# The output projection Wo of an attention kernel, from full fp32 matmuls to three float32r terms, with its units and the FFN rounds at other steps

## The reference

```python
q, k, v = x @ Wq, x @ Wk, x @ Wv                # 16 heads of 64
attn = softmax(causal(q @ k.T / 8))
y = x + concat_heads(attn @ v) @ Wo             # Wo: 1024 x 256
y = layernorm(y, eps=1e-3) * gamma + beta
x = layernorm(x + y)                            # eps 1e-5
h = silu(x @ wg.T) * (x @ wu.T)                 # 768 wide, int weights / 127
out = layernorm(x + h @ wd.T)
```

## Time and profile before

| | |
|---|---|
| median of 3 runs | 1461.75 us (1459.99 to 1463.49) |
| the profiled execution: its own time | 1462.12 us |
| the profiled execution: its span | 1459.7 us |
| mean granted TensorE clock | 0.991 |
| PE, PEld busy | 1403.6 us (96%), 1227.6 us (84%) |
| DVE, ACT, POOL busy | 1014.0, 1003.8, 1003.9 us (69% each) |
| DMA queue q1 | 108.94 MB, 25.0% of 16 engines' span |

### The profile page before, as it was taken

The page is one execution under the profiler, slowest core; times in us unless marked ns, Lnnn a source line. Parts: engine busy times, 40 slices in busy tenths (PEclk is TensorE's granted clock), DMA queues, the critical chain, the costliest instruction groups (busy, mean ns, idle before and its releaser), DMA issues.

```text
span 1459.7 us, 23745 instructions
## 1 busy us (share of the span) xinstructions
PE 1403.6 (96%) x7936; PEld 1227.6 (84%) x7936; DVE 1014.0 (69%) x2729; ACT 1003.8 (69%) x1924; POOL 1003.9 (69%) x944
## 2 busy tenths in 40 slices
PE   6999999999999999999999999999999999999876
PEld 5788888888888888888888888888888888888766
DVE  7766666766666676776667676776766667677874
ACT  4776777767676676766668676686867668676534
POOL 4676766666686775868668586785868668587744
PEclk9999999999999999999999999999999999999988
DMA  4333222312342221321232122132223223122000
GB/s 135 97 81 96 64 60 95 116 52 68 108 131 72 61 88 53 90 85 44 88 116 95 52 59 68 59 117 55 78 66 102 88 59 95 52 59 59 23 11 30
DMA packets 61241, 110.45 MB, mean 76 GB/s; under 512 B 16256, under 2 KB 41600, under 8 KB 61120
## 3 DMA queue, kind: packets, MB, share of 16 engines
q1 hardware_dynamic: 61120, 108.94, 25.0%
HBM read 60.95 MB, written 13.89 MB: 51 GB/s over the span
## 4 chain that ended last, share of the span: by engine, by line
PE 81%; DVE 9%; POOL 4%; ACT 3%; issue 2%; DMA 1%; ACTq 0%; SPq 0%; POOLq 0%
PE bank L787 24%; PE bank L760 16%; PE bank L660 12%; PE bank L736 9%; PE bank L723 7%; PE bank L685 5%; PE bank L822 5%; PE bank L834 3%; POOL probs_lo L1403 2%; DVE K L1121 1%; DVE max_part L1156 1%; POOL h_lo L1445 1%; DVE bank L1154 1%; ACT probs_hi L972 1%; ACT probs L969 1%
## 5 line engine op out<-in xcount | busy, mean ns | idle before, releaser
L1403 POOL TENSOR_TENSOR probs_lo<-probs,probs_hi 128x512 fp32r<-128x512 f32 x576 | 744.1, 1299 | 401.0 <-ACT probs_hi L972 397.8
L969 ACT ACTIVATE probs<-bank 128x512 f32<-128x512 f32 x576 | 344.4, 598 | 304.4 <-DVE bank L1170 219.5
L760 PE MATMUL bank<-Q,K 128*128 128x512 f32 (+3 forms) x1536 | 385.3, 352 | 5.2 <-ACT probs_hi L972 4.5
L972 ACT ACTIVATE probs_hi<-bank 128x512 fp32r<-128x512 f32 x576 | 342.6, 595 | 0.0
L760 PEld LDWEIGHTS bank<-Q,K 128*128 128x128 f32 x1536 | 252.8, 190 | 33.6 <-ACT probs_hi L972 5.7
L736 PE MATMUL bank<-K,Q 128*128 128x512 f32 (+3 forms) x768 | 245.6, 362 | 8.4 <-DVE max_part L1154 6.3
L1154 DVE CUSTOM_DVE_ANT_0 bank<-bank,mask_keys_free 128x128 f32<-128x128 f32 (+3 forms) x512 | 243.3, 506 | 3.4 <-PE bank L736 3.0
L787 PE MATMUL bank<-probs_hi,VH 128*128 128x512 f32 (+3 forms) x768 | 232.0, 343 | 6.0 <-POOL probs_lo L1403 5.3
L787 PE MATMUL bank<-probs_lo,VH 128*128 128x512 f32 (+3 forms) x768 | 234.6, 346 | 0.0
L787 PE MATMUL bank<-probs_hi,VL 128*128 128x512 f32 (+3 forms) x768 | 234.4, 346 | 0.0
L1170 DVE TENSOR_TENSOR bank<-bank,mask_queries_free 128x256 f32<-128x256 f32 (+1 forms) x320 | 119.6, 374 | 148.1 <-PE bank L760 147.0
(11 more groups left out here) (170 smaller groups left out, 2224.3 us busy)
## 6 DMA issues: line engine op xcount, KB each, us to landing
Q<-Q SPq DMA_DIRECT2D x64, 256.0 KB, 3.7
K<-K SPq DMA_DIRECT2D x64, 256.0 KB, 3.4
recip_bc<-recip_scratch SPq DMA_DIRECT2D x62, 256.0 KB, 3.4
wh<-w_scratch SPq DMA_DIRECT2D x12, 768.0 KB, 4.9
wl<-w_scratch SPq DMA_DIRECT2D x12, 768.0 KB, 6.6
wo_quad<-wo SPq DMA_DIRECT2D x16, 256.0 KB, 3.2
y<-x SPq DMA_DIRECT2D x16, 256.0 KB, 3.4
x_tail<-x SPq DMA_DIRECT2D x13, 256.0 KB, 3.1
```

Source lines behind the costliest of these rows:

```text
L760: last = mm(bk[:, at:at + cols], KX[:, n, P * i:P * i + P], QX[:, n, q0:q0 + cols], start=(KX is K1 and at == 0), stop=(KX is K2 and at + ...
L969: A(pe_[:, g % 2, :], stb[g % 2][:, :], ACT.Exp).then_inc(exp_done, 1)
L972: A(ph[:, g % RING, :], stb[g % 2][:, :], ACT.Exp).then_inc(hi_done, 1)
L1403: G.tensor_tensor(pl[:, g % RING, :], pe_[:, g % 2, :], ph[:, g % RING, :].bitcast(F32), ALU.subtract).then_inc(lo_done, 1)
```

## The change

Wo's product is made of float32r matmuls in three terms. ACT rounds the quad's Wo and the normed heads, DVE subtracts for the low parts. The heads' parts of one unit (128x512 each) go into the tail's h_hi and h_lo; in iteration 15, where a tail uses them otherwise, into two pairs of buffers carved from xl. A unit is now 12 matmuls of 128x256. The split of a unit stands one step before the unit on both engines. The units of the iterations 1 to 14 move from the steps 12, 14, 15, 21 to 14, 16, 21, 23; the FFN's rounds in STEADY move from up 9, 23, 29 and down 13, 26, 32 to up 9, 24, 30 and down 12, 27, 33. The load of Wo moves from step 23 to 17 of SP's list, its split stands in step 28. The buffer row_sums goes: its uses go to a row of recip_bc and, at the end, to a mask that is no longer needed, with one more wait each. The last quad's units (after iteration 15) stay fp32.

```diff
-WO_AT, WO_AT_LAST = [12, 14, 15, 21], [11, 13, 15, 16]
+WO_AT, WO_AT_LAST = [14, 16, 21, 23], [11, 13, 15, 16]
+WO_LOAD_AT, WO_SPLIT_AT = 17, 28
...
-STEADY = tail_at(-5, -1, 7, [9, 23, 29], [13, 26, 32], 36)
+STEADY = tail_at(-5, -1, 7, [9, 24, 30], [12, 27, 33], 37)
...
-        rsum, RB = sb("row_sums", [P, S]), sb("recip_bc", [P, S])
+        RB = sb("recip_bc", [P, S])
...
+        WoH, WoL = sb("wo_hi", [P, 2, D], F32R), sb("wo_lo", [P, 2, D], F32R)
...
+        def heads_parts(wi, u):
+            return wo_parts[u % 2] if wi == NIT - 2 else (hh[:, :, :], hl[:, :, :])
...
+        def heads_rows(wi, u):
+
+            a, b = sorted([2 * wi % 3, (2 * wi + 1) % 3])
+            return HT[:, a:b + 1:b - a, 2 * P * u:2 * P * u + 2 * P]
...
-            return (misc[1], misc[0], pvb[0], pvb[1])[u] if wi == NIT - 1 else misc[(1, 1, 0, 1)[u]]
+            return (misc[1], misc[0], pvb[0], pvb[1])[u] if wi == NIT - 1 else misc[(u + 1) % 2]
...
-                src = HT[E:E + 1, h // 2 % 3, :] if h % 2 == 0 else rsum[0:1, :]
+                src = HT[E:E + 1, h // 2 % 3, :] if h % 2 == 0 else RB[E:E + 1, :]
...
-                    sp.wait_ge(wo_mm, 4 * it)
+                    sp.wait_ge(wo_lo, it)
...
-                sp.dma_start(rsum[0:E, CH:S], rscr[HA:HA + 1, 0:CH].partition_broadcast(E).rearrange("e o n -> e (o n)")).then_inc(recip_bc, 16)
+                sp.dma_start(RB[0:E, CH:S], rscr[HA:HA + 1, 0:CH].partition_broadcast(E).rearrange("e o n -> e (o n)")).then_inc(recip_bc, 16)
...
+                if s == WO_LOAD_AT and live:
+                    load_wo(it)
...
                 if s == 23 and live:
                     recip_store(QH * it + 1)
-                    load_wo(it)
                 if s == 24 and live:
                     recip_load(QH * it + 1)
...
-                    pe.wait_ge(y_added, 4 * (it - 2) + 2 + u)
+                    pe.wait_ge(y_added, 4 * (it - 2) + 1 + u)
...
-                elif u == 0 and it >= 2:
-                    pe.wait_ge(y_added, 4 * (it - 1))
+                elif it >= 2:
+                    pe.wait_ge(y_added, 4 * (it - 2) + 3 + u)
...
                 elif u == 1:
-                    pe.wait_ge(y_added, 4 * wi + 1)
-                elif u == 2:
                     if running(it):
                         pe.wait_ge(tdve[0], ND * (it - TAIL_LAG) + DV["y20"])
                     else:
                         pe.wait_ge(v_lo, 4 * it + 4)
                 elif it == NIT - 1:
-                    pe.wait_ge(y_added, 4 * wi + 2)
+                    pe.wait_ge(y_added, 4 * wi + u - 1)
                 else:
-                    pe.wait_ge(proj_lo, 2 * proj_unit(it + 1, 0, 2) + 2)
-                if u == 0:
-                    pe.wait_ge(wo_loaded, 16 * (wi + 1))
-                if u % 2 == 0:
-                    pe.wait_ge(ht_norm, 4 * wi + (1 if it == NIT else 3) + u // 2)
+                    pe.wait_ge(proj_lo, 2 * proj_unit(it + 1, 0, u) + 2)
+                if it == NIT:
+                    pe.wait_ge(wo_loaded, 16 * NIT)
+                else:
+                    pe.wait_ge(heads_lo, 4 * wi + u + 1)
+                    if u == 0:
+                        pe.wait_ge(wo_lo, wi + 1)
                 bk = wo_bank(wi, u)
+
+                hi, lo = heads_parts(wi, u)
                 for t in range(2):
                     tok = P * (2 * u + t)
                     for r in range(2):
-                        last = mm(bk[:, D * t:D * t + D], HT[:, (2 * wi + r) % 3, tok:tok + P], WoS[:, r, :],
-                                  start=(r == 0), stop=(r == 1))
+                        if it == NIT:
+                            last = mm(bk[:, D * t:D * t + D], HT[:, (2 * wi + r) % 3, tok:tok + P], WoS[:, r, :],
+                                      start=(r == 0), stop=(r == 1))
+                        else:
+                            a = heads_at(wi, r)
+                            for n, (X, W) in enumerate(((hi, WoH), (lo, WoH), (hi, WoL))):
+                                last = mm(bk[:, D * t:D * t + D], X[:, a, P * t:P * t + P], W[:, r, :],
+                                          start=(r == 0 and n == 0), stop=(r == 1 and n == 2))
                 last.then_inc(wo_mm, 1)
...
+            def wo_split(it):
+
+                act.wait_ge(wo_loaded, 16 * (it + 1))
+                act.wait_ge(wo_mm, 4 * it)
+                A(WoH[:, :, :], WoS[:, :, :], ACT.Copy).then_inc(wo_hi, 1)
+
+            def heads_split(wi, u):
+                if u % 2 == 0:
+                    act.wait_ge(ht_norm, 4 * wi + 3 + u // 2)
+
+                if wi == NIT - 2:
+                    if u == 0:
+                        act.wait_ge(v_mm, 4 * NIT)
+                    act.wait_ge(wo_mm, 4 * wi + max(u - 1, 0))
+                elif u == 0 and running(wi + 1):
+                    act.wait_ge(tpe[0], NPE * (wi + 1 - TAIL_LAG) + PEC["d0"])
+                else:
+                    act.wait_ge(wo_mm, 4 * wi + u)
+                A(heads_parts(wi, u)[0], heads_rows(wi, u), ACT.Copy).then_inc(heads_hi, 1)
...
                 if (n, c) == (HA, 0):
+
+                    act.wait_ge(mx_read, mx_event_t(NH - 1))
                     act.wait_ge(wo_mm, 4 * (NIT - 1))
                     act.wait_ge(sums_loaded, 16 * (NH - 2))
...
-                    A(rsum[own, cols], pvb[n - HA][other, :], ACT.Copy).then_inc(ht_copied, 1)
+                    A(maskS[own, :], pvb[n - HA][other, :], ACT.Copy).then_inc(ht_copied, 1)
...
                     if c == 0:
                         act.wait_ge(sums_loaded, 16 * h)
+                        act.wait_ge(ht_norm, 2 * pair)
+
                     A(HT[E:P, slot, cols], pvb[c][E:P, :], ACT.Copy)
-                    A(rsum[0:1, cols], pvb[c][0:1, :], ACT.Copy).then_inc(ht_copied, 1)
+                    A(RB[E:E + 1, cols], pvb[c][0:1, :], ACT.Copy).then_inc(ht_copied, 1)
...
+                for u in range(4):
+                    if wo_due(g + 1, u) is not None:
+                        heads_split(wo_due(g + 1, u), u)
                 if 0 <= g < NG:
                     exp(g)
+                if s == WO_SPLIT_AT and 0 <= it < NIT - 1:
+                    wo_split(it)
...
+            def wo_rest(it):
+                dve.wait_ge(wo_hi, it + 1)
+                V.tensor_tensor(WoL[:, :, :], WoS[:, :, :], WoH[:, :, :].bitcast(F32), ALU.subtract).then_inc(wo_lo, 1)
+
+            def heads_rest(wi, u):
+                dve.wait_ge(heads_hi, 4 * wi + u + 1)
+                hi, lo = heads_parts(wi, u)
+                V.tensor_tensor(lo, heads_rows(wi, u), hi.bitcast(F32), ALU.subtract).then_inc(heads_lo, 1)
...
-                V.reciprocal(rsum[:, cols], rsum[:, cols]).then_inc(last_recip, 1)
...
+                V.reciprocal(maskS[:, cols], maskS[:, cols]).then_inc(last_recip, 1)
...
-                V.tensor_tensor(HT[:, slot, cols], HT[:, slot, cols], rsum[:, cols], ALU.mult).then_inc(last_norm, 1)
+                V.tensor_tensor(HT[:, slot, cols], HT[:, slot, cols], maskS[:, cols], ALU.mult).then_inc(last_norm, 1)
...
-                    V.tensor_tensor(HT[0:E, slot, CH:S], HT[0:E, slot, CH:S], rsum[0:E, CH:S], ALU.mult)
+                    V.tensor_tensor(HT[0:E, slot, CH:S], HT[0:E, slot, CH:S], RB[0:E, CH:S], ALU.mult)
...
+                for u in range(4):
+                    if wo_due(g + 1, u) is not None:
+                        heads_rest(wo_due(g + 1, u), u)
+                if s == WO_SPLIT_AT and 0 <= it < NIT - 1:
+                    wo_rest(it)
                 h, k = divmod(g - (C1_DONE + LAG + 2), NS)
                 if k == 0 and 0 <= h < NH - 2:
                     recip(h)
...
```

More of the change, by code:

```diff
@@ L259, in build @@
              Tail(x_tail[:, :, :], c[0], c[1], two(raw[:, 0, :]), c[2], c[3], mxb)]
+        c = carved(xl[:, :, :], 4)
         f_xt = [two(raw[:, 1, :]), two(HT[:, 2, 0:CH]), two(HT[:, 2, CH:S]), x_tail[:, :, :]]
@@ L264, in build, with heads_at @@
              for j, X in enumerate((Q1, Q2, K1, K2))]
+        wo_parts = [(c[0], c[1]), (c[2], c[3])]
+        def heads_parts(wi, u):
[3 more added lines that the diff above has]
+            return HT[:, a:b + 1:b - a, 2 * P * u:2 * P * u + 2 * P]
+        def heads_at(wi, r):
+            return sorted([2 * wi % 3, (2 * wi + 1) % 3]).index((2 * wi + r) % 3)
         def stat(n, g):
@@ L283, in build @@
         sums_loaded, recip_stored, recip_bc = sem("sums_loaded"), sem("recip_stored"), sem("recip_bc_loaded")
-        wo_loaded = sem("wo_loaded")
+        wo_loaded, wo_hi, wo_lo = sem("wo_loaded"), sem("wo_hi"), sem("wo_lo")
+        heads_hi, heads_lo = sem("heads_hi"), sem("heads_lo")
         y_stored, y_inited = [sem(f"y_stored{j}") for j in range(NQ)], [sem(f"y_inited{j}") for j in range(NQ)]
@@ L1307, in last_norm_c1 @@
                     dve.wait_ge(recip_bc, 16 * (NH - 1))
-                    V.tensor_tensor(HT[0:E, slot, CH:S], HT[0:E, slot, CH:S], rsum[0:E, CH:S], ALU.mult)
```

(5 more changed lines are left out.)

## The result

The changed kernel takes 1483.84 us (median of 4 runs, 1481.36 to 1484.12) against 1461.98 for the kernel before on the same chip (1459.99 to 1463.49): a ratio of **1.015, 95% interval 1.0137 to 1.0162**. It is slower by some 22 us; the forecast was 1458, with a range from 1446 to 1467. One execution of all that follow, 2680.24 us for the kernel with round 2 back, stands far outside every other; without it that kernel's median is 1476.51 and not 1476.61.

The account below looks back on a forecast made before the run. PE's own work was taken to set the pace. Against the profiled 1462.12 us, -17.4 + 1.5 + 2.8 + 1.2 + 7.4 + 0.5 = -4.0 gave 1458.1, said as 1458; range for 8 in 10, 1446 to 1467.

Parts of the forecast that it names:

- PE saves, 60 units: Wo units of iterations 1 to 15 on PE: 1.43 us each instead of 1.72, 17.4 us less in all.
- u3's subtraction: DVE's low part for the fourth Wo unit: nearly covered, 0.1 us late on average, 15 times, 1.5 us more.
- rounds 0 and 1, h_lo: PE waits for h_lo before the FFN down-projections: 2.8 us for round 0, 1.2 for round 1, over ten iterations.
- round 2 against the first values unit: Values unit in step 32 needs round 2's h: PE waits 0.74 us in ten iterations, 7.4 us, the largest wait.
- Wo's own split, costed nowhere by itself: Wo's copies on ACT and subtractions on DVE: counted only within the busy sums of 48 and 63 us.
- layernorm one step later: Third layernorm leaves steps 33 to 35, with ACT busy without a gap: costed at 0, bounds -0.5 and +0.3 each.
- iteration 15 and the end: Split of u0 in step 10 makes exp and h of round 0 late: 0.5 us once; the end 0.
- u3's tie: DVE's subtraction for u3 and POOL's probs_lo of step 22 start in the same moment; taken at 0.1 us, ends 0 and 0.6.
- rival "slower": DVE's subtraction and POOL block one another at u2 and u3: 1466 us if one always loses 0.6, 1475 if both; chance 0.16.
- its own cover of 0.4: u3's subtraction was to end at 744.17 and PE to ask for it at 744.58, 0.4 us later.
- Its sum for an iteration with a tail: Ten iterations with a tail change about nothing: 1.16 us against 1.27 each.
- the second least trusted: The layernorm's move, costed at 0, named as the step trusted least after the slack of u3.

## Why the prediction was wrong

By its own terms, in us:

```
step of the prediction                     foretold  trace of after             undone, it gave back
PE saves, 60 units                           -17.4   -17.4 (0.29 us a unit)     -
u3's subtraction                              +1.5   +13.4 (14 x 0.96)          11.3, 12.6
rounds 0 and 1, h_lo                          +4.0   +3.0 (5.2 less [rows 3])   -
round 2 against the first values unit         +7.4   +7.6 (10 x 0.76)           7.4
Wo's own split, costed nowhere by itself       0     +7.0 (5 x 1.3 to 1.55)     1.4 + 6.1
layernorm one step later                       0      in the next row           0
row sums in another buffer                     0     +3.3 (10 x 0.12 to 0.38)   3.9 in the kernel before
iteration 15 and the end                      +0.5   +2.5 (1.7 + 1.16 - 0.37)   -
```

The third column sums to 19.4, of 21.9 measured; 2.5 are not placed. The units of iteration 15 are in the first row with their saving, so 1.16 comes back in the last, and its step 3 is among the ten of the row sums.

**The step that failed is the pricing of u3's tie.** The prediction let the two start "in the same moment" and then took the mean of two outcomes. The schedule repeats from iteration to iteration, and the tie fell the same way in all 14, so there was no mean. And its price was taken from a pair in which DVE came 0.62 after POOL (1.23 long). Those rows already held the rule: DVE ended at 287.96, 0.56 after POOL's 287.40. All the blocked subtractions here end 0.55 after POOL's end, so one that starts together with POOL takes 1.1 longer, not 0.6. The Trainium skill, SBUF — State Buffer, section Who interferes with whom, calls the access exclusive and the later one fully blocked; the trace agrees in that: 1.80 against 0.69. The prediction's estimate from it was 1.3 late, nearer to the 1.11 measured than the 0.6 of the row, which it chose. The rival "slower" had the mechanism and the chance of 0.16; with 1.1 of block and its own cover of 0.4 it would have read 15 x 0.7 for that place, 1467. The cover itself was foretold well: free, the subtraction would have ended at 753.84 + 0.69 = 754.53, and PE would have come to it at some 754.89 (the last of `pv` starts at 754.66, one comes 0.23 after the other), 0.36 later against 0.4 foretold. What the cover left out is that PE started 0.15 after DVE's end (755.64 to 755.79) and that its second matmul came 0.19 after the first, not 0.12. So 1.11 - 0.36 + 0.15 + 0.07 = 0.97 was lost.

**The second is the Wo split**, which stood only in the sums of busy time. The prediction asked of each split of heads what stood behind it, and not of this one: a step with no side work on PE, and the mask of a diagonal tile queued behind on DVE.

**The third is the row sums.** "The end only changes buffers: 0" covers the end alone; the copies of the odd heads were given no price and no bounds.

The working of round 2 held: 0.74 foretold, 0.76 measured in step 32, 7.4 us with it undone. So did the unit (1.43 us, 12 matmuls) and, taken together, the waits for h_lo: 0.16 in round 0, where 0.28 was foretold, and 0.14 more in round 1, where it was 0.12. Its sum for an iteration with a tail, 1.27, is 1.24 by its own terms, which changes nothing. The layernorm's 0 is right by luck: it rested on an ACT that is busy without a gap, and in the trace ACT is idle 0.79 us in step 0 and the work comes later, which costs nothing only because the row sums had made step 3 long already. That step was the second least trusted, and my reading of the trace after the result blamed it wrongly until round 2 was put back.

## What to carry to other kernels

A moved or added DVE operation with two SBUF operands has to be placed against GpSimd's timeline: here it ended 0.55 us (for 128x512) after the GpSimd operation that had started before it, and in a schedule that repeats a tie can be lost every time, as here in 14 of 14. An engine's busy share does not price a small added operation; the first thing queued behind it does, and steps without side work on PE are where that shows. When a change costs more than its terms, undo them one at a time: one of the causes here was in another engine and buffer than the one that the step lengths had pointed to.

## What the runs showed of the hardware

- With both operands in SBUF, DVE's subtraction takes 0.68 to 0.69 us free, and its end behind POOL's is fixed: 753.84 + 1.80 against 753.81 + 1.28, 747.59 + 1.12 against 746.86 + 1.30, each 0.55. It did not matter how late DVE had come, from 0.03 us behind POOL's start (1.80 long) over 0.47 (1.37) to 0.73 (1.12). With one operand from PSUM it runs beside POOL at 0.68.
- Behind the start of an ACT copy of one row of 512 from PSUM partition 0 to SBUF partition 64 the next ACT operation starts 0.61 us later, with SBUF partition 0 as the target 0.49 to 0.50. The buffer was the same in both; other partitions were not tried.
- Twelve float32r matmuls of 128x256 with heads as stationary tiles take 1.43 us, the same as values units. The fp32 units they replace also hold their successor: without streaming, their own steps are 0.1 and the steps behind them 0.2 us longer (3.05 and 1.69 against 2.94 and 1.51).
